# A third written order for the even and odd steps of a pipelined attention kernel

## What is computed

```python
q, k, v = (x @ w_lat @ w_heads for each of q, k, v)   # 16 heads of 8
att = jnp.einsum('bhqd,bhkd->bhqk', q, k) * SCALE
att = jax.nn.softmax(jnp.where(causal, att, -jnp.inf), axis=-1)
y = jnp.einsum('bhqk,bhkd->bhqd', att, v)
x = x + _layernorm(y @ w_proj + b_proj)
x = x + _layernorm(ffn(_layernorm(x)))      # a shared expert and 12 routed ones, two per row
```

## Time and profile before

| | |
|---|---|
| median of 3 runs | 1138.73 us (1134.33 to 1139.64) |
| profiled execution | 1140.07 us, span 1138.3 us |
| busy share of the span | PE 88%, DVE 72%, ACT 66%, POOL 56% |
| two-pass attention | about 60 to 555 us of the span |
| loop of 13 passes | about 101 to 486 us of the span |

### The profile page before, as it was taken

One profiled execution on the slowest core, in us unless ns is written; L12 is line 12 of the kernel. 1 busy time (PEld: TensorE's weight loads), 2 busy tenths in 40 slices (PEclk: granted clock), 3 DMA queues, 4 the chain that ended last, 5 costly groups with the idle time before them and its releaser, 6 DMA issues. The chain is left out here.

```text
span 1138.3 us, 31487 instructions
## 1 busy us (share of the span) xinstructions
PE 1003.8 (88%) x8446; PEld 616.1 (54%) x8446; DVE 824.6 (72%) x2411; ACT 747.5 (66%) x1311; POOL 632.6 (56%) x1195
## 2 busy tenths in 40 slices
PE   4589999999999999978879998659999999999875
PEld 3453434434343444333456664338888888888632
DVE  5688888888888888867688995325666666665637
ACT  4578788888888888856546664316666666666626
POOL 4337777777777777754217777742444444444344
PEclk9899999999999999989968998869999999999988
DMA  8313333333333333342341111132222222221176
GB/s 221 102 30 110 106 111 110 106 108 112 110 105 108 105 106 112 112 125 73 102 160 52 56 54 55 50 82 54 62 64 66 58 67 59 64 62 51 41 240 206
DMA packets 135606, 107.47 MB, mean 94 GB/s; under 512 B 32203, under 2 KB 127874, under 8 KB 135538
## 3 DMA queue, kind: packets, MB, share of 16 engines
q1 hardware_dynamic: 124722, 87.45, 27.2%
q0 software_dynamic: 8544, 17.78, 4.3%
q10 hardware_dynamic: 2272, 1.45, 0.5%
HBM read 55.96 MB, written 50.69 MB: 94 GB/s over the span
## 5 line engine op out<-in xcount | busy, mean ns | idle before, releaser
L1670 DVE TENSOR_REDUCE maxima<-ps 128x8 f32<-128x1024 f32 x320 | 380.1, 1222 | 78.6 <-PE ps L1230 71.2
L945 ACT ACTIVATE pT_area<-ps 128x1024 f32<-128x1024 f32 x320 | 321.1, 1023 | 87.6 <-PE ps L1262 82.2
L840 POOL DMA_INDIRECT ys_dram<-quad_area,place_cur x139 | 133.1, 957 | 193.4 <-issue 138.2
L718 POOL TENSOR_SCALAR_AFFINE_SELECT pT_area<-pT_area 128x256 f32<-128x256 f32 (+1 forms) x448 | 186.5, 439 | 93.6 <-ACT pT_area L945 91.2
L1309 PE MATMUL ps<-pT_area,quad_area 128*32 128x512 f32 (+3 forms) x2048 | 187.5, 450 | 0.6 <-POOL pT_area L718 0.6
L830 POOL DMA_INDIRECT xs_dram<-quad_area,idx_cur x128 | 123.0, 961 | 76.7 <-issue 74.3
L1262 PE MATMUL ps<-quad_area 64*128 64x256 bf16 (+3 forms) x1024 | 127.1, 304 | 29.6 <-DMA quad_area<-mT_sb 27.5
L1529 PE MATMUL ps<-quad_area 128*128 128x256 f32 (+1 forms) x456 | 129.9, 367 | 7.2 <-issue 3.8
L1230 PE MATMUL ps<-quad_area 61*128 61x128 bf16 (+2 forms) x1792 | 127.4, 241 | 4.7 <-ACT pT_area L945 2.7
L1530 PE MATMUL ps<-quad_area 128*128 128x256 f32 (+1 forms) x456 | 128.4, 363 | 0.0
L1089 ACT ACTIVATE xnT<-ps,be_cur 128x256 f32<-128x256 f32 (+1 forms) x228 | 94.7, 447 | 47.4 <-PE ps L1530 47.0
(11 more groups left out here) (237 smaller groups left out, 1528.9 us busy)
## 6 DMA issues: line engine op xcount, KB each, us to landing
qk_dram<-split_area SPq DMA_DIRECT2D x192, 128.0 KB, 2.3
quad_area<-qk_dram SPq DMA_DIRECT2D x256, 96.0 KB, 2.2
row_area<-xs_dram SPq DMA_DIRECT2D x63, 132.0 KB
pT_area<-ys_dram SPq DMA_DIRECT2D x16, 512.0 KB, 5.2
pT_area<-in_L_ffn_We SPq DMA_DIRECT2D x12, 384.0 KB, 7.6
out_dram<-pT_area SPq DMA_DIRECT2D x7, 512.0 KB, 2.9
xs_dram<-row_area SPq DMA_DIRECT2D x5, 528.0 KB, 4.0
split_area<-in_L_ffn_We SPq DMA_DIRECT2D x12, 192.0 KB, 3.6
```

The source lines that it names most:

```text
L718: return pool.affine_select(out=blocks, in_=blocks, compare_op=ALU.is_ge, fill=0.0, base=0, pattern=[[0, count], [1, P]], channel_multipli ...
L840: pool.indirect_dma_start(ys_dram, at, ys[:, ns % 2, h, :], None).then_inc(s_yst[ns % 2], 16)
L945: act.activation(pT[:, gs % 2, n, :], ps[:, bank:bank + 2, :].rearrange("p a b -> p (a b)"), ACT.Exp).then_inc(s_exp, 1)
L1670: dve.tensor_reduce(to, ps[:, bank:bank + 2, :].rearrange("p a (j k) -> p a j k", k=P), AX, ALU.max).then_inc(s_mxf, 1)
```

## The change

Only the order of the attention's steps changes: the tables at lines 83 to 88 and the lists of PE, DVE, ACT and POOL. Every instruction stays; SP's list is the same in both. The core of the diff:

```diff
-EVEN_ITEMS = (("exp", 1), ("max", 3), ("project", None), ("max", 4), ("exp", 4), ("max", 0), ("exp", 2), ("exp", 0), ("max", 1), ("exp", 3), ("max", 2))
-ODD_ITEMS = (("exp", 1), ("max", 2), ("exp", 2), ("max", 4), ("exp", 4), ("max", 0), ("exp", 3), ("max", 3), ("max", 1), ("exp", 0))
+EVEN_ITEMS = (("exp", 4), ("max", 4), ("project", None), ("max", 0), ("exp", 0), ("exp", 2), ("max", 3), ("max", 1), ("exp", 1), ("max", 2), ("exp", 3))
+ODD_ITEMS = (("max", 3), ("exp", 2), ("max", 0), ("exp", 3), ("max", 4), ("exp", 4), ("max", 1), ("exp", 0), ("max", 2), ("exp", 1))
...
                 elif gs % 2 == 0:
+                    probabilities(gs, g, 4)
+                    copy_rows(gs, g)
+                    probabilities(gs, g, 0)
+                    probabilities(gs, g, 2)
+                    copy_max_rows(gs, g)
                     probabilities(gs, g, 1)
-                    copy_rows(gs, g)
+                    probabilities(gs, g, 3)
+                else:
+                    copy_pair(gs, g)
+                    probabilities(gs, g, 2)
+                    probabilities(gs, g, 3)
                     copy_max_rows(gs, g)
                     probabilities(gs, g, 4)
-                    probabilities(gs, g, 2)
                     probabilities(gs, g, 0)
-                    probabilities(gs, g, 3)
-                else:
                     probabilities(gs, g, 1)
...
```

More of the change, by code:

```diff
@@ L82 @@
 RING = 3
-EVEN_ITEMS = (("exp", 1), ("max", 3), ("project", None), ("max", 4), ("exp", 4), ("max", 0), ("exp", 2), ("exp", 0), ("max", 1), ("exp", 3), ("max", 2))
-ODD_ITEMS = (("exp", 1), ("max", 2), ("exp", 2), ("max", 4), ("exp", 4), ("max", 0), ("exp", 3), ("max", 3), ("max", 1), ("exp", 0))
[L85 to L88, removed]
+EVEN_ITEMS = (("exp", 4), ("max", 4), ("project", None), ("max", 0), ("exp", 0), ("exp", 2), ("max", 3), ("max", 1), ("exp", 1), ("max", 2), ("exp", 3))
+ODD_ITEMS = (("max", 3), ("exp", 2), ("max", 0), ("exp", 3), ("max", 4), ("exp", 4), ("max", 1), ("exp", 0), ("max", 2), ("exp", 1))
+MAX_ORDER = ((4, 0, 3, 1, 2), (3, 0, 4, 1, 2))
+EXP_ORDER = ((4, 0, 2, 1, 3), (2, 3, 4, 0, 1))
+MASK_ORDER = ((4, 2, 0, 1, 3), (2, 3, 4, 0, 1))
+PRODUCT_ORDER = ((0, 2, 3, 1), (1, 3, 2, 0))
 AHEAD = {"max": 2, "exp": 0, "max_rows": 1, "turn_back": -2}
@@ L800, in step @@
                     mask_unit(gs, g, 4)
+                    mask_unit(gs, g, 2)
+                    mask_unit(gs, g, 0)
+                    mask_unit(gs, g, 1)
                     next_v(gs, g)
-                    mask_unit(gs, g, 2)
-                    mask_unit(gs, g, 1)
-                    mask_unit(gs, g, 0)
+                    split_maxima(gs, g)
                     mask_unit(gs, g, 3)
-                    split_maxima(gs, g)
                 else:
@@ L809, in step @@
                     mask_unit(gs, g, 2)
+                    split_rows(gs, g, 0)
+                    split_rows(gs, g, 1)
+                    mask_unit(gs, g, 3)
+                    mask_unit(gs, g, 4)
+                    mask_unit(gs, g, 0)
                     mask_unit(gs, g, 1)
[L811 to L814, removed]
+                    split_rows(gs, g, 2)
                     split_maxima(gs, g)
-                    mask_unit(gs, g, 3)
-                    split_rows(gs, g, 2)
             quad_steps(pool, step)
@@ L1364, in step @@
                 elif gs % 2 == 0:
-                    by_key(gs, g, 1)
+                    by_key(gs, g, 4)
+                    most(gs, g, 4)
+                    project_next(gs, g)
+                    most(gs, g, 0)
+                    by_key(gs, g, 0)
+                    first_turn(gs)
+                    products(gs - 1, g - 1, 1)
+                    products(gs - 1, g - 1, 3)
+                    by_key(gs, g, 2)
                     most(gs, g, 3)
-                    project_next(gs, g)
@@ L1368, in step @@
-                    most(gs, g, 4)
                     products(gs - 1, g - 1, 2)
                     turn_maxima(gs, g)
+                    most(gs, g, 1)
+                    by_key(gs, g, 1)
+                    first_projection(gs)
+                    most(gs, g, 2)
+                    products(gs - 1, g - 1, 0)
+                    by_key(gs, g, 3)
+                else:
+                    most(gs, g, 3)
+                    products(gs - 1, g - 1, 0)
+                    by_key(gs, g, 2)
+                    most(gs, g, 0)
+                    by_key(gs, g, 3)
+                    first_turn(gs)
+                    products(gs - 1, g - 1, 2)
+                    most(gs, g, 4)
+                    turn_maxima(gs, g)
@@ L1371, in step @@
                     by_key(gs, g, 4)
[L1372 to L1375, removed]
+                    most(gs, g, 1)
                     products(gs - 1, g - 1, 3)
                     by_key(gs, g, 0)
[L1378 to L1381, removed]
                     most(gs, g, 2)
-                else:
+                    turn_back(gs, g)
@@ L1384, in step @@
                     by_key(gs, g, 1)
[L1385 to L1389, removed]
-                    products(gs - 1, g - 1, 1)
[L1391 to L1400, removed]
+                    products(gs - 1, g - 1, 1)
                 if gs == TAIL + 1:
@@ L1716, in step @@
                 elif gs % 2 == 0:
-                    take_maxima(gs, g, 3)
                     take_maxima(gs, g, 4)
                     take_maxima(gs, g, 0)
+                    take_maxima(gs, g, 3)
                     take_maxima(gs, g, 1)
@@ L1723, in step @@
                 else:
+                    take_maxima(gs, g, 3)
+                    take_maxima(gs, g, 0)
+                    take_maxima(gs, g, 4)
+                    take_maxima(gs, g, 1)
                     take_maxima(gs, g, 2)
[L1725 to L1728, removed]
                     denominators(gs, g)
```

6 lines of the change are left out of this document (removed).

## The result

| | before | after |
|---|---|---|
| median of four runs | 1138.99 us (1134.33 to 1139.64) | **1163.53 us** (1162.28 to 1170.39) |
| profiled execution, span | 1140.07 us, 1138.3 us | 1164.04 us, 1162.3 us |
| busy share of the span | PE 88%, DVE 72%, ACT 66%, POOL 56% | PE 87%, DVE 71%, ACT 65%, POOL 54% |

The changed kernel is **slower: ratio 1.0224, 95% interval 1.0193 to 1.0255**. The forecast was 1165 us.

The account below looks back on a forecast made before the run. PE, nearly full, idles at gates waiting for row DMAs that SP issues one after another. Loop +18.1, clock +10.2, outside -2 make +26.3 us on 1140.07, so 1166.4, less 1.3 for the median: 1165 us, range 1148 to 1184.

Parts of the forecast that it names:

- Even gate to row DMAs: In even steps of the loop, the row DMAs would be issued 5.26 us after PE's gate, the turn coming 2.03 us later.
- SP's lists: Shortest times SP's serial issues need from even to odd row DMAs: 8.07 us q0 to q1, 6.58 us q2 to q3.
- Row DMAs to gate: From issue of an odd step's row DMAs to the next even step's gate on PE: 2.90 us.
- Gate to gate: Between successive even gates in the loop: 16.23 us over q0 and q1, 14.74 us over q2 and q3.
- The pass without a fall: Four steps of the loop at full granted clock: 30.97 us instead of 29.58, 1.39 us more.
- Edits costed at nothing: New ring order and reordered exponentials, masks and maxima in the loop: no cost, since PE, DVE needs stay under 14.74 us.
- The clock: Granted clock falling after longer PE idle time behind q1: 6 of 13 passes at 1.7 us, +10.2 us.
- The loop: The 13 passes, at 1.39 us more each, +18.1 us before the clock falls are added.
- Outside of the loop: Steps behind the loop, whose gates wait 7.5 us in five places: a gain of 2 us, taken as -2.
- SP's list does not bind: Rival for the loop: rows go out when copied, a pass takes 28.2 us, 1119 us in all; chance 0.08.
- the landing costs less: Rival: SP's wait for store landings, 1.08 us a pass, goes; pass 29.89 us, 1141 us in all; chance 0.07.
- A fall in each pass: Rival: the granted clock falls in every loop pass, +22.1 us, +38.2 in all, 1177 us; chance 0.15.

Follow-up runs that it names:

- the turn half way: The changed kernel with the even turn moved up behind exp 2 and its row copy behind exponential 0; 1141.47 us, ratio 1.0022.

## Why the prediction was right

**Direction, size and cause were right.** By its steps:

- *Even gate to row DMAs:* 5.26 us predicted, 301.12 - 295.87 = 5.25 measured.
- *SP's lists:* 8.07 and 6.58 us predicted, 309.17 - 301.12 = 8.05 and 325.32 - 318.74 = 6.58 measured. The rows lay ready for 2.20 and 0.72 us (2.1 and 0.6 predicted).
- *Row DMAs to gate:* 2.90 us predicted, 312.13 - 309.17 = 2.96 measured.
- *Gate to gate:* 16.23 and 14.74 us predicted; 16.26, and 14.62 from 344.45 to 359.07. The pass without a fall, 30.97 predicted, is 30.90.
- *Edits costed at nothing:* they cost nothing in the loop; with the turn early the new order runs at 29.01 us a pass. Odd gates hide their wait, as said, and that is worth more than I gave it: in the kernel before, whose odd gates stand first, the late turn costs 41 us. PE's idle time in the pass without a fall is 30.90 - 28.39 = 2.5 us (some 3 predicted).

**The terms that were mis-sized.** *The clock:* I took 6 falls in 13 passes at 1.7 us; it was 9 in 13, one of them in the first pass, at about 1.5 (32.4 - 30.9). The 6 was a choice between none and 13, so that it came this near is luck. *The loop* came to +31.1 us instead of 28.3: 12.5 x 1.32 = 16.5 for the passes, 7 x 1.5 = 10.5 for the falls that lie between the first pass and the last projection, and some 4 that are nearly all of the first pass. That one took 34.3 us: its gate at 120.47 idled 3.45 us, which I did not foresee, and the clock fell behind it. *Outside of the loop* I took -2 us, and the profile shows +1.5 ahead of it and -8.6 behind. In steps 54 to 65 (4.3 us less) the gate waits for its row DMAs 0.8 us in one place, where it waited 7.5 us in five, so most of that wait went; other idle times of PE took some of it back, the longest 3.2 us at L1230, for which the profile names no releaser. The rest is behind the attention, where the instructions are the same, and whose length varies between 574.4 and 579.4 us over the thirteen profiles; I don't count it as an effect. The errors are of opposite sign, so the total came closer than its terms, and that too is luck.

**The rivals.** That SP's list does not bind fell with the row DMAs at 309.12 to 309.17, and with the one added issue. That the landing costs less fell by the 13.3 us of after; it can be made to cost less, but only by another list. A fall in each pass was four too many: there were nine in thirteen.

The word "bound" needs care in hindsight. From 309.17 to 325.32 SP issues for 1.61 + 2.18 + 1.86 + 1.62 + 2.16 + 1.99 = 11.42 of 16.15 us, 71%. By the Trainium skill (Perfetto Trace Analysis, What "DMA-bound" means) a kernel is bound by the DMA sequencer where the issuing engine's track is solid with DMA slices. SP's track has gaps in every step here, and yet an issue more lengthens the pass: what counts is the list between one step's rows and the next, in a ring of gate, turn, copy, row DMAs and gate.

## What to carry to other kernels

Where two results that alternate go out through one in-order queue, write down the shortest time that the queue needs between them, and compare it with the distance that the order of the producer leaves; to make one earlier and the other later costs as soon as the second distance is under it. Move the queue's list together with the producer's: put what is ready ahead of what comes late, and make sure that it is ready by then (here POOL's split, which 1.4 us were enough to spoil). An order should be judged with the list that suits it: this change lost 2.2% with the old list and wins 1.2% with another, which in the old order loses 5.6%.

## What the runs showed of the hardware that was not expected

- The price of an issue on SP does not follow its bytes. By the durations shown, divided by the number of issues, it is 0.8 us for a row DMA of 6 KB, 0.6 for the added 12 KB, but 0.47 to 0.50 for a load of 96 KB and 0.73 for a store of 128 KB.
- Idle times of 1.92 to 1.98 us ahead of a gate, alike to 0.06 us, were followed by a fall of the granted clock in eight of twelve passes and not in four. The order is regular: one pass without a fall, then two with one, four times over. In the first of the two the gate still takes 0.39 to 0.40 us (184.11, 279.76, 375.38, 470.91) and the fall comes behind it; in the second the gate itself takes 0.61 (216.58, 312.13, 407.80, 503.31). With 2.74 to 2.84 us (one issue more) there was a fall in ten of eleven passes. With about 1.05 us (the turn half way) and with four waits of 0.6 to 1.3 us in each pass (the late turn in the kernel before) there was none in the twelve passes behind the first. What sets the order of the four and the eight stays open.
